# Stacks of five chunks made by PE and ACT, and one chunk's look-up moved to the seam of two tiles

## The chip, the core and the metric

The kernel runs on one core of one Trainium2 chip. Its engines are PE (TensorE, matrix products), DVE (VectorE), ACT (ScalarE), POOL (GpSimd) and SP (SyncE, which here only issues DMAs). The metric is the device time of one execution in microseconds (us), lower is better.

## What is computed

A recommendation tower for 2048 rows: 39 table look-ups of 32 numbers, a bilinear form for each of the 741 pairs of fields, and a three-layer perceptron.

```python
e = jnp.stack([tbl_0[ids[:, 0]], ..., tbl_38[ids[:, 38]]], axis=1)   # 2048 x 39 x 32
p = inputs[:, ROW, :]                                                # inputs is e; ROW < COL, all pairs
q = inputs[:, COL, :]
z = jnp.einsum('bpc,apc,bpa->bp', p, w, q)                           # w: 32 x 741 x 32
h = jnp.concatenate([z, dense_ctx], axis=1)                          # 741 + 16 columns
h = jnp.maximum(h @ W_top1 + b_top1, 0.0)
h = jnp.maximum(h @ W_top2 + b_top2, 0.0)
y = h @ W_top3
```

## The kernel before

The 2048 rows are four tiles of 512 (tile 0 to 3). The 39 fields are ten chunks of four (chunk 9 has three). A chunk of a tile is written (tile, chunk), as (1, 8).

**Units and batches.** The pairs are 200 units per tile. A unit is one PE product of a weight block with the stack of one field j (`interact`, L593), multiplied by DVE with the plain form of a chunk (`multiply`, L914, two units at a time: one product, 100 per tile), and summed into z by PE (`reduce`, L617). Two products make a batch; there are 50 batches per tile, and this document numbers them through, so that batch 69 is batch 19 of tile 1. PE's order in a batch is: the four matmuls of `interact`, pieces of the perceptron of the tile before (L630, L632), `reduce` of the batch before, then a turn or look-ups for chunks to come.

**How a chunk is brought.** Either its rows are gathered by POOL, one DMA for each field and 128 rows (L422), and turned by PE (`turn`, L537); or it is looked up: DVE makes one-hot rows of the indices (L902), one slice at a time, and PE multiplies them with the table (`look_up`, L556; 12 matmuls for a full slice of four fields, ten slices for chunks 1, 7 and 8). Both end in the PSUM buffer `t_ps`, which has one place. ACT then copies it twice (`take_chunk`, L720 and L725): a rounded high part `parts`, and the plain form `eT`. DVE subtracts for the low part (`split_chunk`, L868).

**How a stack is made.** `interact` needs for each field both parts repeated over all 128 partitions, in `e4`. SP does it through DRAM: `store_parts` writes the high part (L467) and the low part (L469) to `scratch`, and `stack_chunk` reads them back, repeated (L480, two DMAs of 512 KB), after it has waited for both stores. All of it stands in SP's one queue, with the pieces of the weights (L439) and the indices (L459). For the first chunks of tile 0 (`MADE`: chunks 1, 0, 2, 3, 7) it is done without DRAM: `make_half` (L574) multiplies the parts with a repeating matrix into PSUM, two fields at once, and ACT copies the result into `e4` (L735 to L738).

**What sets the order.** Tables written by hand: `FIRST_TILE` and `OTHER_TILES` give for each chunk the batch of its turn, or one batch for each slice of its look-up (batches of 50 and more are those of the next tile). The stores and stacks follow from the batch in which the chunk is complete: the store one batch later, the stack two batches later (three or four in tile 0), but not before the stack that has the place in `e4` is used up. `UNITS` sets when a stack is first needed: chunk 1 and 0 in batch 0 of a tile, 2 in batch 2, 3 in batch 5, 7 in batch 9, 4 in batch 14, 8 in the second product of batch 19, 5 in 28, 6 in 36, 9 in 42. POOL's gathers each wait, up to number 96, for the landing of the third gather before; after that they are paced by the products done.

**Places in `eT`.** Chunks 0, 1, 2, 3 and 7 have two, so the next tile's can be written while this tile's is still in use; the others have one, and wait for the last product of the tile before.

Of the kernel before, what the change touches and what calls it, by code (L numbers as in the profile page):

```python
# [5 lines left out]
P = 128  # L6
F = 39
D = 32
# [13 lines left out]
def fields_in(g):  # L22
    return min(C, F - C * g)
# [72 lines left out]
def place_sums():  # L96
# [3 lines left out]
    for (g, gi, j), quad in zip(UNITS, map(int, QUADS)):  # L100
# [4 lines left out]
        if quad == 0 and D * (NZ - 1) <= row < D * (NZ - 1) + DENSE:  # L105
# [20 lines left out]
OS = 3  # L126
PR = 4

TWO_PLACES = (0, 1, 2, 3, 7)

# [11 lines left out]
FIRST_TILE = ((2, 0, 0, (0, 0, 0, 1, 1, 1, 1, 1)), (7, 0, None, (1, 1, 1, 2, 2, 2, 2, 2, 2, 2)), (3, 0, 3, ()), (4, 0, 7, ()),  # L142
# [3 lines left out]
OTHER_TILES = ((8, 0, None, (0, 1, 1, 2, 3, 4, 4, 5, 6, 6)), (4, 0, 7, ()),  # L146
# [3 lines left out]
LAST_TABLE_BATCH = 2  # L150

MADE = ((0, 1), (0, 0), (0, 2), (0, 3), (0, 7))
MADE_FIRST = 2
MADE_IN = {1: (((0, 2), 0), ((0, 2), 1)), 4: (((0, 3), 0), ((0, 3), 1)), 5: (((0, 7), 0),), 6: (((0, 7), 1),)}
MLP_WEIGHTS_BATCH = 7
LATE = (17, 39)
# [32 lines left out]

def stores_to(n):  # L190

    return len([m for m in range(n + 1) if (m - n) % 2 == 0 and ORDER[m] not in MADE])


def halves_before(c, half):
# [34 lines left out]
    INDICES.setdefault(LAST_SLICE.get(LOOKED[LPOS[c] - 2], -1) + 1, []).append(c)  # L230
for b, cs in COMPLETE.items():
    for c in cs:
        if c in MADE:
            continue
        x = e4_before(c)
        free = NBAT * x[0] + J_LAST[x[1]] // UPB + 1 if x else 0

        late = LATE[0] <= b < LATE[1]
        STORES.setdefault(b + 1 + late, []).append(c)
        STACKS.setdefault(max(b + (4 if late else 3 if b < LATE[0] else 2), free), []).append(c)  # L240
# [43 lines left out]
def tower(nc, tables, ids, hot_ids, hot_rows, dense, w, w1, b1, w2, b2, w3, sel_in, ident_in, y):  # L284
# [4 lines left out]
    with ExitStack() as ctx:  # L289
# [229 lines left out]
        def _(pe):  # L519
# [42 lines left out]
            def make_half(c, half):  # L562
# [12 lines left out]
                                                start=h == 0, stop=h == 1)  # L575
                last.then_inc(s_stk, 1)

            def interact(t, n):
                s = NS * t + n
                if s >= 2:  # L580
                    pe.wait_ge(s_mul, s - 1)
                slots = [e_slot(t, UNITS[UPS * n + i][1]) for i in range(UPS)]
                for i in range(UPS):
                    u = UPS * n + i
                    g, gi, j = UNITS[u]
                    if u == J_FIRST[g]:
                        pe.wait_ge(s_e4[E4_SLOT[g]], 32 * e4_loads((t, g)))
                    if u % PW == 0:
                        p = NPW * t + u // PW
                        pe.wait_ge(s_w4[p % WR], 16 * (p // WR + 1))  # L590
                    place = i if slots[0] <= slots[1] else 1 - i
                    p = NPW * t + u // PW
                    last = nc.tensor.matmul(u_ps[:, s % 2, place, :], w4[:, p % WR, (u % PW) * P:(u % PW + 1) * P],  # L593
                                            e4[:, E4_SLOT[g], j - C * g, :], start=True, stop=True)
                last.then_inc(s_u, 1)
# [86 lines left out]
            for t in range(NT):  # L682
                for b in range(NBAT):
                    for x in range(SPB):
                        interact(t, SPB * b + x)
                    if t:
                        for piece in mlp_pieces(b, t == NT - 1):
                            mlp_piece(t - 1, *piece)
                    if b:
                        reduce(t, b - 1)  # L690
                    elif t:
                        reduce(t - 1, NBAT - 1)
                    for c in TURNS.get(NBAT * t + b, ()):
                        turn(c)
                    for c, k in TAKES.get(NBAT * t + b, ()):
                        look_up(c, k)
                    if t == 0:
                        for c, half in MADE_IN.get(b, ()):
                            make_half(c, half)
                    if t == NT - 1:  # L700
                        for m, k in EARLY.get(b, ()):
                            early_piece(t, m, k)
# [3 lines left out]
        def _(act):  # L706
            def take_chunk(c):
# [1 line left out]
                n = POS[c]  # L709
                rows = D * fields_in(g)  # L710
                if n >= 2:
                    if ORDER[n - 2] in MADE:
                        act.wait_ge(s_stk, 2 * MADE.index(ORDER[n - 2]) + 2)
                    else:
                        act.wait_ge(s_scr[n % 2], 32 * stores_to(n - 2))
                if hot(c):
# [9 lines left out]

            def take_half(c, half):
                made = MADE.index(c)
                act.wait_ge(s_stk, 2 * made + half + 1)
                x = e4_before(c)  # L730
                if x:
                    act.wait_ge(s_u, step_after(*x))
# [3 lines left out]
                else:  # L736
                    nc.scalar.copy(e4[:, slot, q, :], m_ps[:, :]).then_inc(s_e4[slot], 8)
                    nc.scalar.copy(e4[:, slot, q + 1, :], z_ps[:, 1, :]).then_inc(s_e4[slot], 8)  # L738

            def load_weights(k):  # L740
                a, b = PREP_UNITS[k]
# [86 lines left out]
            for t in range(NT):  # L828
                for b in range(NBAT):
                    if t:  # L830
                        for layer, m, k in mlp_pieces(b, t == NT - 1):
                            if k == LAYER_INPUTS[layer] - 1:
                                take_mlp(t - 1, layer, m, m_ps[:, :])
                    for tile in range(NZ):
                        done = ends_tile(tile) // UPB + 1
                        if done == b:
# [189 lines left out]
```

## Time and profile before

| | |
|---|---|
| median of 3 runs | 739.4 us (738.17 to 740.45) |
| the profiled execution: its own time | 739.08 us |
| its span, first to last instruction | 737.2 us |
| PE busy | 678.2 us, 92% |
| DVE busy | 608.3 us, 83% |
| ACT busy | 104.3 us, 14% |
| POOL busy | 415.6 us, 56% |

The two busiest engines are PE and DVE, and they hand work to each other in every batch. A mean share hides the stages: the profile's 40 slices show PE at 6 to 9 tenths in the first twelve or so, and at 9 in nearly all that follow, while the share of the DMA engines is highest in the slices from 74 to 203 us. The span is 1.9 us shorter than the execution's own time.

### The profile page before, as it was taken

The page shows a single profiled execution, that of the slowest core. Times are in us where ns is not written, and L with a number is a line of the kernel's source. Part 1 is how long each engine was busy: PE and PEld are TensorE (multiplying, and loading weights), DVE is VectorE, ACT ScalarE, POOL GpSimd, SP SyncE. Part 2 cuts the span into 40 slices and gives each one's busy share as a digit, 9 for nine tenths or more (in the row PEclk, how much of TensorE's full clock was granted, in tenths as well). Part 3 has the DMA queues.
Part 4 walks back from the last instruction along what each step waited for, and adds up shares of the span by engine and source line. Part 5 has one row for each costly group of instructions (what it writes and reads, how often), then busy time and mean ns, then how long its engine had stood idle before and what let it go on. Part 6 is the DMA issues. An engine that isn't in the chain of part 4 may idle for free.

```text
span 737.2 us, 10924 instructions
## 1 busy us (share of the span) xinstructions
PE 678.2 (92%) x4202; PEld 274.6 (37%) x4202; DVE 608.3 (83%) x773; ACT 104.3 (14%) x186; POOL 415.6 (56%) x424
## 2 busy tenths in 40 slices
PE   0678886898997999999999999999999999999998
PEld 0233332333333444434344444433434444343443
DVE  3776797799996998898889997998889978788740
ACT  3423301111110010101211010110110101011002
POOL 5777465567777766567766665567766666000000
PEclk9888999899998999999999999999999999999999
DMA  7644979779876573547675582728686373553200
GB/s 200 209 119 138 334 272 301 252 231 314 284 227 202 195 257 108 166 140 236 224 225 192 202 281 68 240 85 259 194 270 214 125 254 98 179 174 104 97 0 0
DMA packets 72271, 141.40 MB, mean 192 GB/s; under 512 B 13829, under 2 KB 23704, under 8 KB 72092
## 3 DMA queue, kind: packets, MB, share of 16 engines
q1 hardware_dynamic: 48796, 116.86, 46.2%
q10 hardware_dynamic: 9984, 16.94, 6.4%
q0 software_dynamic: 13440, 6.91, 6.4%
q8 instruction: 33, 0.54, 0.3%
q14 instruction: 18, 0.15, 0.1%
HBM read 109.66 MB, written 31.00 MB: 191 GB/s over the span
## 4 chain that ended last, share of the span: by engine, by line
PE 70%; DVE 14%; issue 7%; DMA 4%; POOL 3%; ACT 1%; SPq 0%; DVEq 0%; ACTq 0%
PE u_ps L593 23%; PE z_ps L617 21%; DVE prod L914 9%; PE m_ps L630 8%; PE t_ps L556 7%; DVE one_hot L902 4%; POOL e_rows L422 3%; PE m_ps L632 3%; PE t_ps L537 2%; DMA e<-scratch 1%; DMA e_rows<-in_tbl_dram,idx 1%; PE u_ps L652 1%; PE u_ps L661 1%; PE m_ps L634 1%; PE t_ps L644 1%
## 5 line engine op out<-in xcount | busy, mean ns | idle before, releaser
L422 POOL DMA_INDIRECT e_rows<-in_tbl_dram,idx x420 | 415.4, 989 | 212.9 <-issue 89.9
L914 DVE TENSOR_TENSOR prod<-u_ps,eT 128x1024 f32<-128x1024 f32 x400 | 469.5, 1216 | 77.6 <-PE u_ps L593 77.1
L593 PE MATMUL u_ps<-e,w 128*128 128x512 f32 x800 | 260.9, 437 | 24.6 <-DVE prod L914 14.6
L617 PE MATMUL z_ps<-prod,sel 128*32 128x512 f32 x1600 | 222.9, 614 | 0.0
L593 PEld LDWEIGHTS u_ps<-e,w 128*128 128x128 f32 x800 | 132.2, 190 | 173.4 <-DVE prod L914 85.9
L902 DVE TENSOR_SCALAR one_hot<-hot_idx,row 125x512 bf16<-125x512 f16 (+2 forms) x296 | 107.6, 420 | 9.6 <-PE t_ps L556 5.8
L556 PE MATMUL t_ps<-one_hot,tb 125*32 125x512 bf16 x1344 | 104.2, 392 | 10.5 <-DVE one_hot L902 9.1
L556 PEld LDWEIGHTS t_ps<-one_hot,tb 125*32 125x32 bf16 x1344 | 43.7, 99 | 89.3 <-issue 57.6
L617 PEld LDWEIGHTS z_ps<-prod,sel 128*32 128x32 f32 x1600 | 33.8, 108 | 111.7 <-issue 87.4
L630 PE MATMUL m_ps<-zT,w1s 128*128 128x512 f32 x144 | 73.5, 592 | 0.0
L720 ACT CAST parts<-t_ps 128x512 fp32r<-128x512 f32 (+1 forms) x40 | 23.4, 586 | 295.4 <-PE t_ps L556 162.4
L868 DVE TENSOR_TENSOR parts<-eT,parts 128x512 fp32r<-128x512 f32 (+1 forms) x40 | 27.3, 683 | 3.2 <-ACT eT L725 3.2
L630 PEld LDWEIGHTS m_ps<-zT,w1s 128*128 128x128 f32 x144 | 27.2, 189 | 6.4
L791 ACT ACTIVATE h<-m_ps,b1s 128x512 f32<-128x512 f32 x13 | 9.0, 689 | 145.1 <-PE m_ps L630 143.9
L784 ACT COPY zT<-z_ps 128x512 f32<-128x512 f32 x24 | 14.1, 586 | 102.9 <-PE z_ps L617 102.9
L537 PE MATMUL t_ps<-ident,e_rows 128*128 128x128 f32 (+2 forms) x112 | 19.2, 296 | 6.6 <-DMA e_rows<-in_tbl_dram,idx 6.6
L632 PE MATMUL m_ps<-h,w2s 128*128 128x512 f32 x48 | 24.5, 592 | 0.0
L725 ACT COPY eT<-t_ps 128x512 f32<-128x512 f32 (+1 forms) x40 | 23.7, 591 | 0.0
L537 PEld LDWEIGHTS t_ps<-ident,e_rows 128*128 128x128 f32 (+2 forms) x112 | 12.2, 142 | 30.3 <-issue 27.1
L875 DVE TENSOR_TENSOR h<-h 128x512 fp32r<-128x512 f32 (+1 forms) x13 | 8.7, 668 | 2.7 <-ACT h L751 2.7
L751 ACT CAST h<-h 128x512 fp32r<-128x512 f32 (+1 forms) x13 | 7.9, 609 | 17.2 <-DMA h<-in_w_dram 17.2
L632 PEld LDWEIGHTS m_ps<-h,w2s 128*128 128x128 f32 x48 | 9.0, 188 | 2.1
(52 smaller groups left out, 122.2 us busy)
## 6 DMA issues: line engine op xcount, KB each, us to landing
w<-w_rows SPq DMA_DIRECT2D x100, 512.0 KB
e<-scratch SPq DMA_DIRECT2D x62, 512.0 KB, 5.7
scratch<-parts SPq DMA_DIRECT2D x62, 256.0 KB
w_rows<-h ACTq DMA_DIRECT2D x48, 256.0 KB
e_rows<-in_tbl_dram,idx POOLq DMA_INDIRECT x420
hot_idx<-hot SPq DMA_DIRECT2D x12, 512.0 KB
h<-in_w_dram ACTq DMA_DIRECT2D x12, 256.0 KB, 4.3
e<-scratch SPq DMA_DIRECT2D x8, 384.0 KB
```

The lines of the kernel that those rows point to most:

```text
L422: pool.indirect_dma_start(e_rows[:, r, n, D * q:D * q + D], None, tables[f], bass.IndirectOffsetOnAxis(ap=idx[:, t, f * TPG + n:f * TPG + ...
L537: last = nc.tensor.transpose(t_ps[0:hi, b * P:b * P + P], rows, ident[:, :])
L556: last = nc.tensor.matmul(t_ps[D * q:D * q + D, :], tb[0:HP, part, col:col + D], one_hot[0:HP, n % OS, here * NB:(here + 1) * NB], start=k ...
L593: last = nc.tensor.matmul(u_ps[:, s % 2, place, :], w4[:, p % WR, (u % PW) * P:(u % PW + 1) * P], e4[:, E4_SLOT[g], j - C * g, :], start=T ...
L617: last = nc.tensor.matmul(z_ps[D * quad:D * quad + D, z % 2, :], sel[:, D - 1 - row:2 * D - 1 - row], prod[:, (NS * t + n) % PR, place, :] ...
L630: last = nc.tensor.matmul(m_ps[:, :], w1s[:, k, m * P:m * P + P], zT[:, t % 2, k, :], start=k == 0, stop=stop)
L632: last = nc.tensor.matmul(m_ps[:, :], w2s[:, k, m * P:m * P + P], h1[:, k, :], start=k == 0, stop=stop)
L720: nc.scalar.copy(parts[0:rows, n % 2, 0, :], t_ps[0:rows, :]).then_inc(s_eh, 1)
L725: nc.scalar.copy(eT[0:rows, e_slot(t, g), :], t_ps[0:rows, :]).then_inc(s_et, 1)
L868: nc.vector.tensor_tensor(parts[0:rows, n % 2, 1, :], eT[0:rows, e_slot(t, g), :], parts[0:rows, n % 2, 0, :].bitcast(F32), ALU.subtract). ...
L902: last = nc.vector.tensor_scalar(one_hot[0:HP, n % OS, i * NB:(i + run) * NB], hot_idx[0:HP, LPOS[c] % 2, x * NB:(x + run) * NB], (row10 i ...
L914: nc.vector.tensor_tensor(prod[:, s % PR, :, :], u_ps[:, s % 2, :, :], e, ALU.mult).then_inc(s_mul, 1)
```

## The change

Three things are changed.

1. The stacks of (0, 4), (0, 8), (0, 5), (0, 6) and (0, 9) no longer pass through DRAM. `FIELD_WISE` gives the first batch of each; in that batch and the following ones `make_field` has PE repeat one field by two matmuls into `m_ps`, between `interact` and `reduce`, and `take_field` has ACT copy it into `e4`. That is 19 fields in batches 9 to 12, 15 to 18, 21 to 24, 30 to 33 and 35 to 37.
2. The look-up of the next tile's chunk 7 moves to batches 46 to 52 (48 to 52 in tile 0), where it was in 20 to 27 (32 to 38). In the other tiles chunk 8 moves behind chunk 4, from batches 0 to 6 to batches 8 to 15, and the others by some batches: the turn of chunk 5 from 19 to 16, chunk 9 from 36 to 34, the next tile's chunk 2 from 39 to 37, 0 from 43 to 41, 3 from 49 to 45; the look-up of the next tile's chunk 1 from 8 to 17 to 17 to 26.
3. Chunk 7 has one place in `eT`.

```diff
-TWO_PLACES = (0, 1, 2, 3, 7)
+TWO_PLACES = (0, 1, 2, 3)
...
-              (7, 1, None, (32, 32, 33, 33, 34, 35, 35, 36, 37, 38)), (2, 1, 40, ()), (0, 1, 43, ()), (3, 1, 48, ()))
-OTHER_TILES = ((8, 0, None, (0, 1, 1, 2, 3, 4, 4, 5, 6, 6)), (4, 0, 7, ()),
...
+              (2, 1, 40, ()), (0, 1, 43, ()), (3, 1, 48, ()), (7, 1, None, (48, 49, 49, 49, 50, 50, 51, 51, 52, 52)))
+OTHER_TILES = ((4, 0, 7, ()), (8, 0, None, (8, 9, 10, 10, 11, 12, 13, 13, 14, 15)), (5, 0, 16, ()),
...
+FIELD_WISE = {(0, 4): 9, (0, 8): 15, (0, 5): 21, (0, 6): 30, (0, 9): 35}
+STACKED = MADE + tuple(FIELD_WISE)
...
 for b, cs in COMPLETE.items():
     for c in cs:
-        if c in MADE:
+        if c in STACKED:
             continue
...
+            def make_field(c, q):
+
+                n = POS[c]
+                pe.wait_ge(s_el, n + 1)
+                d = c if q else STACKED[STACKED.index(c) - 1]
+                pe.wait_ge(s_e4[E4_SLOT[d[1]]], 32 * e4_loads(d) - (32 - 8 * q if q else 0))
+                own = slice(D * q, D * q + D)
+                for h in range(2):
+                    last = nc.tensor.matmul(m_ps[:, :], rep[own, 2 - 2 * h:2 - 2 * h + P], parts[own, n % 2, h, :],
+                                            start=h == 0, stop=h == 1)
+                last.then_inc(s_stk, 1)
...
                     for x in range(SPB):
                         interact(t, SPB * b + x)
+                    if t == 0:
+                        for c, q in field_in(b):
+                            make_field(c, q)
...
+            def take_field(c, q):
+                act.wait_ge(s_stk, stk_at(c, q))
+                act.wait_ge(s_u, step_after(*e4_before(c)))
+                slot = E4_SLOT[c[1]]
+                rest = 8 if q < fields_in(c[1]) - 1 else 32 - 8 * q
+                nc.scalar.copy(e4[:, slot, q, :], m_ps[:, :]).then_inc(s_e4[slot], rest)
```

**Place 1: PE in tile 0, the batches from 15.** `u_ps` is the result of `interact`, `z_ps` that of `reduce`, `m_ps<-parts,rep` a repeated field. Before:

```order
L593 MATMUL u_ps<-e,w 128x512 x4
L617 MATMUL z_ps<-prod,sel 32x512 x4
L593 MATMUL u_ps<-e,w 128x512 x4
L617 MATMUL z_ps<-prod,sel 32x512 x4
L593 MATMUL u_ps<-e,w 128x512 x4
```

In the changed kernel:

```order
L622 MATMUL u_ps<-e,w 128x512 x4
L603 MATMUL m_ps<-parts,rep 128x512 x2
L646 MATMUL z_ps<-prod,sel 32x512 x4
L622 MATMUL u_ps<-e,w 128x512 x4
L603 MATMUL m_ps<-parts,rep 128x512 x2
L646 MATMUL z_ps<-prod,sel 32x512 x4
L622 MATMUL u_ps<-e,w 128x512 x4
L603 MATMUL m_ps<-parts,rep 128x512 x2
```

Batch 15 and batch 16 have each got the two matmuls of one field of chunk 8 between `interact` and `reduce`, and so have 17 and 18.

**Place 2: SP in tile 1, from the first store of (1, 8).** `scratch<-parts` is a store, `e<-scratch` a stack's read, `hot_idx<-hot` the indices of a look-up, `w<-w_rows` a piece of the weights. Before, the second pair of stores is that of (1, 4):

```order
L467 DMA scratch<-parts 128x512 [waits s_eh]
L469 DMA scratch<-parts 128x512 [waits s_el]
L459 DMA hot_idx<-hot 128x2048 [waits s_hot]
L467 DMA scratch<-parts 128x512 [waits s_eh]
L469 DMA scratch<-parts 128x512 [waits s_el]
L480 DMA e<-scratch 64x4x512 [waits s_scr1,s_u]
L480 DMA e<-scratch 64x4x512
```

In the changed kernel, the second pair is that of (1, 5):

```order
L484 DMA scratch<-parts 128x512 [waits s_eh]
L486 DMA scratch<-parts 128x512 [waits s_el]
L456 DMA w<-w_rows 128x1024 [waits s_u]
L476 DMA hot_idx<-hot 128x2048 [waits s_hot]
L484 DMA scratch<-parts 128x512 [waits s_eh]
L486 DMA scratch<-parts 128x512 [waits s_el]
L497 DMA e<-scratch 64x4x512 [waits s_scr0,s_u]
L497 DMA e<-scratch 64x4x512
L497 DMA e<-scratch 64x4x512 [waits s_scr1,s_u]
L497 DMA e<-scratch 64x4x512
```

The order is the same but for one piece of the weights: the stack of (1, 8) stands behind both stores of the next chunk, and the next chunk's stack follows at once.

**Place 3: PE, from the last slice of chunk 8's look-up.** `t_ps<-one_hot,tb` is a look-up, `t_ps<-ident,e_rows` a turn, `m_ps<-zT,w1s` a piece of the perceptron. Before, in tile 2, where the row of 18 is the end of the look-up of (2, 8), in batch 106:

```order
L556 MATMUL t_ps<-one_hot,tb 32x512 x18
L593 MATMUL u_ps<-e,w 128x512 x4
L630 MATMUL m_ps<-zT,w1s 128x512
L617 MATMUL z_ps<-prod,sel 32x512 x4
L537 MATMUL t_ps<-ident,e_rows 128x128 x4
L593 MATMUL u_ps<-e,w 128x512 x4
L630 MATMUL m_ps<-zT,w1s 128x512
L617 MATMUL z_ps<-prod,sel 32x512 x4
L556 MATMUL t_ps<-one_hot,tb 32x512 x12
L593 MATMUL u_ps<-e,w 128x512 x4
L630 MATMUL m_ps<-zT,w1s 128x512
```

In the changed kernel, in tile 1, where the two rows of 9 are its end, in batches 64 and 65:

```order
L573 MATMUL t_ps<-one_hot,tb 32x512 x9
L622 MATMUL u_ps<-e,w 128x512 x4
L659 MATMUL m_ps<-zT,w1s 128x512
L646 MATMUL z_ps<-prod,sel 32x512 x4
L554 MATMUL t_ps<-ident,e_rows 128x128 x4
L622 MATMUL u_ps<-e,w 128x512 x4
L659 MATMUL m_ps<-zT,w1s 128x512
L646 MATMUL z_ps<-prod,sel 32x512 x4
L573 MATMUL t_ps<-one_hot,tb 32x512 x12
L622 MATMUL u_ps<-e,w 128x512 x4
L659 MATMUL m_ps<-zT,w1s 128x512
L646 MATMUL z_ps<-prod,sel 32x512 x4
L573 MATMUL t_ps<-one_hot,tb 32x512 x12
L622 MATMUL u_ps<-e,w 128x512 x4
```

The batches behind the look-up hold the same work. What moved is the first use of the stack: before it is in batch 119, thirteen batches behind the row of 18; now it is in the last row shown, four batches behind the second row of 9 (the third and fourth matmul of that `interact`).

## Rows read from the trace of the kernel before

**Rows 1.** Windows: stretch, length, busy (count) of PE, PEld, DVE, ACT, POOL; PEclk, DMA.
```profile
39.40:234.00 194.60, 165.31 (x1146) 62.01 (x1145) 167.79 (x226) 31.32 (x56) 130.27 (x128) 0.93 0.74 246
234.00:395.50 161.50, 160.85 (x1023) 67.12 (x1022) 145.58 (x182) 18.49 (x33) 107.09 (x112) 1.00 0.62 197
...
127.40:134.20 6.80, 3.17 (x11) 0.89 (x12) 1.94 (x4) 0.00 (x0) 3.53 (x4) 0.50 0.74 262
...
226.40:233.20 6.80, 4.98 (x17) 2.50 (x18) 3.00 (x4) 1.07 (x2) 4.97 (x7) 0.50 0.40 135
```

**Rows 2.** Waits, whole run: engine, line, cause, total us, times, longest.
```profile
PE u_ps L593 <- DMA e<-scratch: 5.8, 1, 5.8
```

**Rows 3.** Windows of product L914: stretch, length, busy (count), clock, DMA.
```profile
125.40:135.10 9.70, 2.56 (x3) 0.65 0.82 302
175.50:198.80 23.30, 16.39 (x14) 1.00 0.92 317
201.70:212.20 10.50, 9.32 (x8) 1.00 0.59 184
```

**Rows 4.** Timeline at 119 to 132 us: start, length, engine, line, operation.
```profile
119.64 1.35 SPq L480 DMA_DIRECT2D e<-scratch  x2
...
131.03 1.19 PE L593 MATMUL u_ps<-e,w 128*128 128x512 f32 x2 [5.76 <-DMA e<-scratch]
```

**Rows 5.** Timeline at 221 to 229 us.
```profile
221.96 0.94 POOL L422 DMA_INDIRECT e_rows<-in_tbl_dram,idx  x1 [0.30 <-issue]
...
228.22 1.09 PE L537 MATMUL t_ps<-ident,e_rows 128*128 128x128 f32 x4 [4.13 <-DMA e_rows<-in_tbl_dram,idx]
```

**Rows 6.** Gathers L422, 4 to 159 us: wait, total us, times.
```profile
  DMA e_rows<-in_tbl_dram,idx: 33.0, 25
```

**Rows 7.** Timeline at 81 to 83 us: stacks made by PE.
```profile
81.98 0.50 PE L574 MATMUL m_ps<-parts,rep 32*128 32x512 f32 x1
...
82.65 0.73 PE L593 MATMUL u_ps<-e,w 128*128 128x512 f32 x2
```

**Rows 8.** Chain of waits at 266 us: start, length, work.
```profile
266.77 0.99 PE z_ps L617 x8
267.77 0.65 PE t_ps L556 x12
```

**Rows 9.** Timeline at 256 to 269 us: chunk 8 of tile 1.
```profile
256.29 1.48 PE L556 MATMUL t_ps<-one_hot,tb 125*32 125x512 bf16 x18
...
261.45 0.32 SPq L469 DMA_DIRECT2D scratch<-parts  x1
...
264.54 0.68 DVE L868 TENSOR_TENSOR parts<-eT,parts 128x512 fp32r<-128x512 f32 x1
...
265.13 1.01 DVE L902 TENSOR_SCALAR one_hot<-hot_idx,row 125x512 bf16<-125x512 f16 x3
...
268.35 1.21 PE L593 MATMUL u_ps<-e,w 128*128 128x512 f32 x4
```

**Rows 10.** Stack line L480 at 265 us: issues, issue to landing.
```profile
L480 SPq DMA_DIRECT2D e<-scratch x2: 592/615/638, 265.7 to 266.3; - x2
...
DMA to landing us min/median/max: 5.5/6.1/6.7
```

**Rows 11.** L480 at 427 us, and PE's timeline at 430 us.
```profile
L480 SPq DMA_DIRECT2D e<-scratch x2: 592/614/637, 427.7 to 428.3; - x2
...
DMA to landing us min/median/max: 5.0/5.4/5.9
...
430.34 1.21 PE L593 MATMUL u_ps<-e,w 128*128 128x512 f32 x4
```

**Rows 12.** L480 at 589 us, and PE's timeline at 591 us.
```profile
L480 SPq DMA_DIRECT2D e<-scratch x2: 592/608/625, 589.3 to 590.0; - x2
...
DMA to landing us min/median/max: 5.2/5.6/5.9
...
591.12 1.20 PE L593 MATMUL u_ps<-e,w 128*128 128x512 f32 x4
```

More of the change, by code:

```diff
@@ L144 @@
               (1, 1, None, (20, 21, 22, 22, 23, 24, 25, 25, 26, 27)), (6, 0, 28, ()), (9, 0, 31, ()),
[1 row of a table removed]
-OTHER_TILES = ((8, 0, None, (0, 1, 1, 2, 3, 4, 4, 5, 6, 6)), (4, 0, 7, ()),
[3 rows of a table removed]
[1 row of a table added]
+OTHER_TILES = ((4, 0, 7, ()), (8, 0, None, (8, 9, 10, 10, 11, 12, 13, 13, 14, 15)), (5, 0, 16, ()),
+               (1, 1, None, (17, 18, 19, 20, 21, 22, 23, 24, 25, 26)), (6, 0, 28, ()), (9, 0, 34, ()),
+               (2, 1, 37, ()), (0, 1, 41, ()), (3, 1, 45, ()), (7, 1, None, (46, 47, 47, 48, 49, 49, 50, 51, 51, 52)))
 LAST_TABLE_BATCH = 2
@@ L190, in stores_to, with stk_at, stk_after, field_in @@
 def stores_to(n):
-    return len([m for m in range(n + 1) if (m - n) % 2 == 0 and ORDER[m] not in MADE])
+    return len([m for m in range(n + 1) if (m - n) % 2 == 0 and ORDER[m] not in STACKED])
+def stk_at(c, part):
+    earlier = STACKED[:STACKED.index(c)]
+    return sum(2 if x in MADE else fields_in(x[1]) for x in earlier) + part + 1
+def stk_after(c):
+    return stk_at(c, (2 if c in MADE else fields_in(c[1])) - 1)
+def field_in(b):
+    return [(c, b - first) for c, first in FIELD_WISE.items() if first <= b < first + fields_in(c[1])]
 def halves_before(c, half):
@@ L711, in take_chunk @@
                 if n >= 2:
-                    if ORDER[n - 2] in MADE:
-                        act.wait_ge(s_stk, 2 * MADE.index(ORDER[n - 2]) + 2)
+                    if ORDER[n - 2] in STACKED:
+                        act.wait_ge(s_stk, stk_after(ORDER[n - 2]))
                     else:
@@ L728, in take_half @@
                 made = MADE.index(c)
-                act.wait_ge(s_stk, 2 * made + half + 1)
+                act.wait_ge(s_stk, stk_at(c, half))
                 x = e4_before(c)
@@ L833, in _ @@
                                 take_mlp(t - 1, layer, m, m_ps[:, :])
+                    if t == 0:
+                        for c, q in field_in(b):
+                            take_field(c, q)
                     for tile in range(NZ):
```

3 rows, old and new, of the table OTHER_TILES are left out of this document.

## The prediction

> **What bounds the kernel now.** I read first the windows by tile, then the list of waits, then the timeline at each long wait, and last the timeline where the work stands that the change moves.
>
> The windows show two regimes [rows 1]. In tile 1 (tiles 2 and 3 are alike) PE is busy for all but 0.7 us, at a granted clock of 1.00, which is 2.4 GHz: PE bounds, and a wait of PE there is added to the time in full. Tile 0 takes 194.6 us against 161.5 for tile 1, though no perceptron runs beside it. So tile 0 has something to give back.
>
> The waits say that PE waits for a stack's DMA once in the whole run [rows 2]. The timeline shows where: at the second product of batch 19, the first use of chunk 8, PE stands idle 5.76 us until 131.03; its stack was issued at 119.64 [rows 4]. A second idle of 4.13 us ends at 228.22: the turn of (1, 3) in batch 48 waits for its last gather, issued at 221.96, with POOL issuing back to back at 0.30 us gaps [rows 5]. After each of the two the clock is at 0.50, 1.2 GHz, for 6.8 us [rows 1]: it fell 2.1 us after the first idle began (125.3) and 2.3 us after the second (224.1).
>
> **The change, part by part.** The sum is made against the profiled execution's own time, 739.1 us (span 737.2), which is 0.3 under the median of the runs.
>
> *Chunk 8's stack in tile 0.* The stretch from the first product of batch 19 to that of batch 20 is 9.7 us [rows 3]. A batch with little beside it takes 10.5 / 4 = 2.6 (the stretch 201.7 to 212.2, eight products). The fourth field is made in batch 18, with a `reduce` and two matmuls between it and its use, so nothing is late: 7.1 us go, the half clock among them.
>
> *Nineteen fields on PE.* A `make_half` puts four matmuls on PE in 82.65 - 81.98 = 0.67 us; `m_ps` and `z_ps` run side by side there [rows 7]. A single field is two matmuls behind one another in the same row group, so 0.67 as well: 12.7 us if all of it shows. But in tile 0 DVE is the busier engine (167.8 against 165.3 us), and in 2.6 us of a light batch PE has some 2.1 of work: `reduce` is 0.99 [rows 8], and the four matmuls of `interact` 1.1 to 1.2 [rows 9]. With a field it needs 2.8. So some 0.2 to 0.4 us shows for each, and next to nothing where slices of a look-up keep DVE busy at 1.01 each [rows 9]. I take 0.3: +5.7 us, between 0 and 12.7. The 19 copies cost nothing: ACT is busy 31.3 of 194.6 us.
>
> At this place the Trainium skill speaks against the change. "TensorEngine Tiling", Key Properties, says that changing the tiling mode, not merely the tile, drains TensorE; each field has 32 rows between work of another shape, so two such changes each. By the rule 38 drains would be added; as one matmul is reported at 0.50 us and its half of the 0.67 is 0.34, that is 0.16 each, 6.1 us, and the sum below would be 757. The trace does not show it: the row at 82.65 begins with no gap behind the fields [rows 7].
>
> *The look-up of (1, 7) leaves batches 32 to 38.* They take 23.3 us for seven; at 2.6 they would be 18.2: -5.1.
>
> *The turn of (1, 3).* It would be wanted at 224.1 - 7.1 - 5.1 + 5.7 = 217.6. For that its gathers must come 10 us sooner. Of the first 96 gathers 25 waited for landings, 33.0 us in all [rows 6], beside the stores and stacks that go (5 x 1.5 MB) and the weights that stay. Bounds are 0 and 33; I take 10, a third of it, since only part of the waits stand beside those stacks. The turn is then at 218.
>
> *The end of tile 0.* From that turn to tile 1's first product (234.0) it is now 5.8 us, 5.0 of them at half clock, of which 2.5 are lost. Added are four slices of (1, 7), at 1.01 us on DVE: 5.8 - 2.5 + 4.0 = 7.3. Tile 1 starts at 225.3: tile 0 gives -8.7 us.
>
> *Looks moved to later tiles.* A full slice of twelve matmuls is 0.65 us of PE [rows 8]. 24 matmuls more fall to tile 1 and 30 to tile 3: 54 x 0.054 = 2.9. At the seams two slices in a batch cost DVE 2.0 beside two products, more than PE's share; but batches 0 to 6 are so filled today. I take +3.0 for all of this, between 0 and 6.
>
> *Chunk 8 in tiles 1 to 3: what is late next.* Now the look-up ends in batch 15 of the tile and the stack is needed in batch 19. Today's trace holds this very sequence, nine batches earlier, with the same work on PE and SP behind it, so the lateness can be read. In tile 1 the look-up ends at 256.29 + 1.48 = 257.8; DVE's split comes behind the next batch's products, and the low part's store is issued at 261.45. The stack stands in SP's queue behind the low store of the next chunk, whose split starts at 264.54 [rows 9]. It is issued at 265.7 and 266.3 and the later one lands 6.7 us after: at 273.0 [rows 10]. The chain takes 15.2 us. PE is at the second product of the fourth batch behind the look-up half way through the row of four at 268.35, at 269.0. Lateness: 4.0 us. In the same way tile 2: 428.3 + 5.9 = 434.2 against 430.9, 3.3 [rows 11]; tile 3: 590.0 + 5.9 = 595.9 against 591.7, 4.2 [rows 12]. Today nobody sees it, since chunk 8 is needed nine batches later. Behind the waiting matmul stand the perceptron's pieces, `reduce`, every look and turn, and DVE waits for u: nothing is caught up in a tile that PE bounds. +11.5 us, between 8 (each later read landing in 5.0 us, the least in these rows) and 16 (the piece of weights that now stands ahead of the stack, up to 1.5 each).
>
> The Trainium skill's "DMA: Bandwidth & Descriptors", Bandwidth, gives 6.15 us for a transfer of 1 MB. The stack is two reads of 512 KB; by that figure it would land at 265.7 + 6.15 = 271.8 in tile 1, 2.9 us late, not 4.0, and the sum would be some 3 us lower. The rows have 7.3 us from the first issue, and they decide.
>
> *The clock behind those stalls.* The two long idles of today were followed by 6.8 us at half, beginning 2.1 to 2.3 us into the idle. A stall of 4.0 would leave 5.0 us of work at half, 2.5 lost; three make 7.5, or 0 if the clock stays. The new stalls are a little shorter than the two in the rows, except by 0.1 in one: I take 2.0 each, +6.0.
>
> **Sum.** 739.1 - 8.7 + 3.0 + 11.5 + 6.0 = 750.9, so 751 us.
>
> **Rivals.** *The stacks are there in time* (faster). If SP reaches them sooner or the tile runs slower up to batch 19, no stall appears and the time is 739.1 - 8.7 + 3.0 = 733. It decides where the chain from the end of the look-up to the landing is under 11 us. For it: in tile 2 the pair landed 6.5 us after the first issue, in tile 1 7.3, so it varies. Against: the two stores and the split alone took 8 us before the first issue, and three rows out of three are late.
>
> *The stalls come, the clock stays*: 739.1 - 8.7 + 3.0 + 11.5 = 745. For: they are short. Against: the clock fell at 2.1 and 2.3 us of idle.
>
> *POOL holds tile 0.* If the gathers get nothing back, the turn of (1, 3) stays at 228, and tile 0 ends at 228 + 7.3 + 2.5 = 238, so 12.5 us more than in my sum: 763; with half of it 757. For: POOL issues there at 0.94 + 0.30 = 1.24 us each [rows 5], which no freed DMA shortens. Against: the 33.0 us of waits.
>
> *The drains*, 757, see above.
>
> *The change does not take the stall of batch 19 away*, since ACT's copies are late. ACT is idle most of the tile, and the last copy has a `reduce` to itself. Then 758.
>
> **Chances.** Forecast (stalls with a falling clock) 0.60, with a range of its own of 746 to 757; stalls with the clock kept 0.15; in time 0.12; POOL 0.08; drains 0.03; the last 0.02. The range of 8 in 10 is 738 to 760: it leaves out most of the rival in time, and the worst of POOL's. A measurement tells 0.3%, 2.2 us, from no change. Faster by over that: 0.13, the rival in time and a little of the kept clock with shorter stalls; within it 0.04; slower 0.83.
>
> **What would show it.** Right: among the waits, PE at `interact` for the stack's DMA three times, 3 to 5 us each, in tiles 1, 2 and 3, at the second product of batches 69, 119 and 169, each with a stretch at clock 0.50; tile 0 at about 186 us, with no stall at batch 19; DVE still the busier one there. Wrong: tiles 1 to 3 without such waits; the turn in batch 48 idle for over 3 us; tile 0 over 192 us, which would say that the fields cost more than 0.3 each.

## The result, and the profile after

The changed kernel takes 756.1 us (median of 4 runs, 753.9 to 759.7). The kernel before, on the same chip, takes 738.8 us (4 runs, 736.8 to 740.5). The ratio is 1.025, with a 95% interval of 1.021 to 1.028. The forecast was 751 us, slower, with a range of 738 to 760. It was 5 us low, which the point-by-point section takes apart.

The profiled execution took 757.1 us, 18.0 more than the one before. The page of the changed kernel, the lines that answer to the numbers shown of before:

```profile
span 755.3 us, 11032 instructions
...
PE 694.4 (92%) x4240; PEld 282.8 (37%) x4240; DVE 610.0 (81%) x773; ACT 115.2 (15%) x205; POOL 412.4 (55%) x424
...
DMA packets 68304, 133.94 MB, mean 177 GB/s; under 512 B 13509, under 2 KB 23384, under 8 KB 68124
...
L622 PE MATMUL u_ps<-e,w 128*128 128x512 f32 x800 | 259.8, 439 | 26.9 <-DMA e<-scratch 13.9
...
L777 ACT CAST e<-m_ps 128x512 fp32r<-128x512 f32 x19 | 11.2, 587 | 60.1 <-PE m_ps L603 59.3
...
L603 PE MATMUL m_ps<-parts,rep 32*128 32x512 f32 x38 | 14.8, 471 | 0.0
```

The engines' shares have hardly moved, and 7.5 MB fewer pass through the DMA engines. Neither tells of a slower kernel. One number in the fifth part does: 13.9 us in which PE waited for stacks. The 19 fields are there as well (L603, L777).

The windows of the changed kernel by tile, then four stretches at half clock (columns as in [rows 1]):

```profile
39.90:228.00 188.10, 172.82 (x1133) 67.22 (x1133) 163.96 (x216) 41.12 (x73) 130.79 (x132) 0.93 0.66 210
228.00:399.40 171.40, 164.34 (x1045) 68.25 (x1043) 147.60 (x185) 18.96 (x33) 104.19 (x108) 0.98 0.60 191
399.40:567.90 168.50, 162.19 (x1023) 67.30 (x1022) 146.87 (x183) 18.97 (x33) 104.23 (x109) 0.99 0.59 190
...
116.80:127.00 10.20, 10.20 (x30) 3.84 (x29) 5.41 (x5) 1.17 (x2) 6.40 (x7) 0.50 0.41 128
297.70:304.50 6.80, 5.82 (x24) 1.87 (x24) 2.14 (x4) 0.00 (x0) 1.20 (x1) 0.50 0.85 308
468.30:471.70 3.40, 3.40 (x12) 1.00 (x14) 2.14 (x4) 0.00 (x0) 1.20 (x1) 0.51 1.05 388
635.60:639.00 3.40, 3.40 (x12) 0.85 (x10) 1.23 (x1) 0.00 (x0) 0.94 (x1) 0.50 0.93 343
```

Tile 0 gave back 6.5 us (194.6 before [rows 1], 188.1 now). Each later tile is longer: tile 1 by 9.9 (161.5 before [rows 1]), tile 2 by 6.5, tile 3, counted to the end of the span, by 7.7 (the table below has all of them). Taken between the first products of the tiles, with 0.5 us before tile 0, that is 0.5 - 6.5 + 24.1 = 18.1.

The stretch of one batch in which the stack of chunk 8 is first needed, from the windows of the product's line: tiles 1, 2 and 3, then tile 0, then the last five batches of tile 1 (stretch, length, busy, clock, DMA share, GB/s):

```profile
293.40:305.30 11.90, 2.43 (x2) 0.71 0.72 259
463.80:473.40 9.60, 2.43 (x2) 0.82 0.90 321
630.90:640.10 9.20, 2.45 (x2) 0.81 0.95 336
132.00:135.20 3.20, 2.36 (x2) 1.00 0.96 277
381.50:399.30 17.80, 11.75 (x10) 1.00 0.62 206
```

In tile 0 that batch took 9.7 us [rows 3] and now takes 3.2: the stall is gone. In the later tiles it took 3.3, 3.3 and 3.4 us in the kernel before and now takes 11.9, 9.6 and 9.2, 20.7 us more in all. The rest of the three tiles is 3.4 us longer. The seam shows on its own: 17.8 us for five batches, where the kernel before has

```profile
381.10:395.40 14.30, 11.69 (x10) 1.00 0.68 215
```

That is 3.5 us more, with two slices of a look-up and two products on DVE in a batch. The first eight batches of tile 1, now free of chunk 8's slices, give 2.6 of it back (28.3 us before, 25.7 after).

The waits of the changed kernel, whole run, which answer to [rows 2]:

```profile
PE u_ps L622 <- DMA e<-scratch: 13.9, 3, 5.4
```

Three waits now stand where there was one of 5.8. The timeline of PE and SP in tile 1, from the end of the look-up of (1, 8) on (start, length, engine, line, operation, idle before it and what ended it). It is the sequence that [rows 9] had nine batches earlier:

```profile
281.17 0.83 PE L573 MATMUL t_ps<-one_hot,tb 125*32 125x512 bf16 x9
...
285.68 0.32 SPq L486 DMA_DIRECT2D scratch<-parts  x1
...
286.04 0.43 SPq L456 DMA_DIRECT2D w<-w_rows  x1
...
286.52 0.46 SPq L476 DMA_DIRECT2D hot_idx<-hot  x1
...
289.47 0.32 SPq L486 DMA_DIRECT2D scratch<-parts  x1
289.88 7.53 SPq L497 DMA_DIRECT2D e<-scratch  x4
...
298.68 1.19 PE L622 MATMUL u_ps<-e,w 128*128 128x512 f32 x2 [5.37 <-DMA e<-scratch]
299.67 1.91 PE L659 MATMUL m_ps<-zT,w1s 128*128 128x512 f32 x2
```

The look-up ends at 282.0, and the low part's store is issued at 285.68. The stack may go only at 289.88, behind the next chunk's low store at 289.47 (of the four reads in that row the first two are this stack, the others the next chunk's). PE stands idle for 5.37 us, and the matmuls that follow take 1.91 us for two where 1.02 is usual. In tiles 2 and 3 the same matmul ends idles of 4.26 and 4.30:

```profile
468.02 0.90 PE L622 MATMUL u_ps<-e,w 128*128 128x512 f32 x2 [4.26 <-DMA e<-scratch]
```
```profile
635.30 0.92 PE L622 MATMUL u_ps<-e,w 128*128 128x512 f32 x2 [4.30 <-DMA e<-scratch]
```

The stack's line in tile 1, which answers to [rows 10]:

```profile
L497 SPq DMA_DIRECT2D e<-scratch x2: 592/712/832, 289.9 to 290.5; - x2
...
DMA to landing us min/median/max: 5.7/6.9/8.0
```

The later of the two reads landed 8.0 us after its issue, at 298.5; it was 6.7 in [rows 10]. The whole chain, end of look-up to landing, is 298.5 - 282.0 = 16.5 us. I had read 15.2 for it.

### The profile page after: what moved, and what is told of

It is laid out like the page before. It is cut to its first block, busy times and chain, and to the rows that moved or that the text cites. A ratio compares the mean times of both kernels' runs of the same rounds, so it can differ in the third digit from the quotient of the medians.

```text
span 755.3 us, 11032 instructions
## 1 busy us (share of the span) xinstructions
PE 694.4 (92%) x4240; PEld 282.8 (37%) x4240; DVE 610.0 (81%) x773; ACT 115.2 (15%) x205; POOL 412.4 (55%) x424
## 4 chain that ended last, share of the span: by engine, by line
PE 67%; DVE 14%; issue 7%; DMA 5%; POOL 4%; ACT 1%; SPq 0%; DVEq 0%; ACTq 0%
PE u_ps L622 22%; PE z_ps L646 20%; DVE prod L956 10%; PE m_ps L659 8%; PE t_ps L573 6%; POOL e_rows L439 4%; DVE one_hot L944 4%; DMA e<-scratch 3%; PE m_ps L661 2%; DMA e_rows<-in_tbl_dram,idx 2%; PE t_ps L554 2%; PE u_ps L681 1%; PE m_ps L603 1%; PE u_ps L690 1%; PE t_ps L673 1%
## 5 line engine op out<-in xcount | busy, mean ns | idle before, releaser
L622 PE MATMUL u_ps<-e,w 128*128 128x512 f32 x800 | 259.8, 439 | 26.9 <-DMA e<-scratch 13.9
L646 PE MATMUL z_ps<-prod,sel 128*32 128x512 f32 x1600 | 225.5, 620 | 0.0
L622 PEld LDWEIGHTS u_ps<-e,w 128*128 128x128 f32 x800 | 134.0, 192 | 174.7 <-issue 89.4
L573 PE MATMUL t_ps<-one_hot,tb 125*32 125x512 bf16 x1344 | 102.1, 387 | 12.0 <-DVE one_hot L944 9.3
L659 PE MATMUL m_ps<-zT,w1s 128*128 128x512 f32 x144 | 76.2, 611 | 0.0
L554 PEld LDWEIGHTS t_ps<-ident,e_rows 128*128 128x128 f32 (+2 forms) x112 | 11.8, 139 | 28.0 <-issue 23.0
L777 ACT CAST e<-m_ps 128x512 fp32r<-128x512 f32 x19 | 11.2, 587 | 60.1 <-PE m_ps L603 59.3
L603 PE MATMUL m_ps<-parts,rep 32*128 32x512 f32 x38 | 14.8, 471 | 0.0
```

Of the source, the lines that this page charges most:

```text
L554: last = nc.tensor.transpose(t_ps[0:hi, b * P:b * P + P], rows, ident[:, :])
L573: last = nc.tensor.matmul(t_ps[D * q:D * q + D, :], tb[0:HP, part, col:col + D], one_hot[0:HP, n % OS, here * NB:(here + 1) * NB], start=k ...
L646: last = nc.tensor.matmul(z_ps[D * quad:D * quad + D, z % 2, :], sel[:, D - 1 - row:2 * D - 1 - row], prod[:, (NS * t + n) % PR, place, :] ...
L659: last = nc.tensor.matmul(m_ps[:, :], w1s[:, k, m * P:m * P + P], zT[:, t % 2, k, :], start=k == 0, stop=stop)
```

## The experiments

Six kernels were run. Two theories were on the table. A: the stack of chunk 8 comes too late in tiles 1 to 3, because its chain has a length of its own and too few batches to fit in, and the clock falls in the wait. B, in several forms: the rest of the change, the moved look-ups, the fields or the traffic, has a good part in it. The table gives all results; "stretch" is the batch in which chunk 8 is first needed. The lengths in it are of the one profiled execution of each kernel. The runs of the kernel before beside the six had medians of 737.9 us (19 runs) and, for the one batch sooner and the filled wait, 738.3 (13). The changed kernel's four runs stand beside the 738.8, so a difference to its median carries up to 0.9 us by which these three differ, and its own spread of 6.

| kernel | median us (runs) | ratio to before, 95% | tiles 0 to 3, us | stretch in tiles 1, 2, 3 |
|---|---|---|---|---|
| before | 738.8 (4) | | 194.6, 161.5, 162.0, 179.6 | 3.3, 3.3, 3.4 |
| changed | 756.1 (4) | 1.021 to 1.028 | 188.1, 171.4, 168.5, 187.3 | 11.9, 9.6, 9.2 |
| chunk 8 three batches sooner | 736.3 (10) | 0.997 to 1.002 | 185.1, 163.2, 161.8, 181.0 | 3.7, 3.7, 3.0 |
| chunk 8 one batch sooner | 739.8 (10) | 0.999 to 1.005 | 190.0, 164.8, 163.6, 182.5 | 4.8, 5.1, 4.5 |
| stack first in SP's queue | 753.0 (4) | 1.017 to 1.027 | 185.2, 166.3, 169.2, 188.3 | 7.0, 8.7, 10.1 |
| wait filled with matmuls | 750.4 (4) | 1.011 to 1.026 | 188.4, 167.7, 166.2, 185.6 | 8.3, 7.7, 7.4 |
| tables alone, no fields | 762.3 (4) | 1.027 to 1.041 | 193.6, 171.6, 167.6, 187.0 | 11.1, 9.2, 8.9 |
| fields alone, old tables | 734.9 (10) | 0.993 to 0.999 | 187.2, 161.4, 162.0, 179.6 | 3.4, 3.4, 3.4 |

**Chunk 8 three batches sooner.** The whole change stays, but in the later tiles chunk 8 is looked up three batches earlier, and the turn of chunk 4 makes room.

```diff
-OTHER_TILES = ((4, 0, 7, ()), (8, 0, None, (8, 9, 10, 10, 11, 12, 13, 13, 14, 15)), (5, 0, 16, ()),
+OTHER_TILES = ((4, 0, 4, ()), (8, 0, None, (5, 6, 7, 7, 8, 9, 10, 10, 11, 12)), (5, 0, 16, ()),
```

> The changed kernel with one table line altered: in tiles 1 to 3 chunk 4 is turned in batch 4 (not 7) and chunk 8 is looked up in batches 5 to 12 (not 8 to 15), so its stack has seven batches, not four, before its first use. Theory A (the loss of the changed kernel is the three waits of PE for chunk 8's stack, 5.4 + 4.3 + 4.3 us, with the half clock behind them): no such wait is left, the stretches from the first product of batches 69, 119 and 169 to the next fall from 11.9, 9.6 and 9.2 us to about 3.4 each, 20 us in all, and the time is 736 (734 to 739). Rival B (the loss is the two slices in a batch at the seams and the dense look-ups, which keep DVE busy): the waits may go but the time stays over 748.

Measured: 736.3 us, and no wait of PE for a stack in the list of waits. The three stretches, windows of the product's line:

```profile
290.00:293.70 3.70, 2.37 (x3) 1.00 0.93 313
452.20:455.90 3.70, 2.39 (x3) 1.00 0.94 325
612.70:615.70 3.00, 2.35 (x2) 1.00 0.67 220
```

This is theory A with its number. One row of a table carries the whole loss: 19.8 us between the medians. The first two of these stretches have a DMA share as high as or higher than in the changed kernel (0.93 against 0.72 in tile 1, 0.94 against 0.90 in tile 2), so a high share in that batch makes no stall by itself.

The row does more than give room. In the changed kernel the stack is issued 4.2, 4.2 and 3.8 us behind its low store, after both stores of the next chunk; here no other chunk's store stands between, and it goes 2.1 us behind. From the low store to the landing of the later read it takes 9.6, 9.6 and 7.3 us in the three tiles, against 12.9, 11.8 and 10.5. So the chain itself is shorter here, and this experiment does not separate the three batches of room from that. The last experiment, a single batch with the next chunk's stores still ahead of the stack, comes nearer to it.

**The stack first in SP's queue.** Within a batch SP now issues the stack before the next chunk's stores.

```diff
-                    for c in STORES.get(NBAT * t + b, ()):
-                        store_parts(c)
                     for c in STACKS.get(NBAT * t + b, ()):
                         stack_chunk(c)
+                    for c in STORES.get(NBAT * t + b, ()):
+                        store_parts(c)
```

> The changed kernel with SP's two loops of a batch swapped: stacks due in a batch are issued ahead of the stores due in it. Theory A (part of the lateness is the place in SP's queue, behind both stores of the next chunk): the stack of chunk 8 is issued as soon as its own low store has landed, about 2.2 us sooner, each of the three waits gets 2.2 us shorter, and the time falls by 6 to 10, to 746 to 750. Rival B (the DMA engines' traffic sets the landing, not the place in the queue): the stack lands when it did, the waits stay at 13.9 us in sum, and the time stays at 756 within 1.5.

Measured: 753.0 us, 3 less than the changed kernel, where 6 to 10 were expected; the medians alone can't tell 3 us here, the traces can. The timeline in tile 1:

```profile
282.38 0.32 SPq L486 DMA_DIRECT2D scratch<-parts  x1
...
284.86 1.25 SPq L497 DMA_DIRECT2D e<-scratch  x2
...
293.25 0.70 PE L622 MATMUL u_ps<-e,w 128*128 128x512 f32 x2 [3.23 <-DMA e<-scratch]
```

The first read goes out 2.5 us behind the low store, not 4.2. It helps only in part: from the low store to the matmul that waits it now takes 10.9, 10.9 and 10.8 us in the three tiles, against 13.0, 11.9 and 10.6 in the changed kernel. In tile 3 nothing was gained. Its place in the queue is worth about 2 us in tile 1 and 1 in tile 2. What remains is two passes through DRAM behind each other; how the 10.8 us divide into the store, the reads and the traffic beside them was not tried. The expectation was half right: the issue came sooner in all three tiles, as theory A had it, and the landing followed in two.

Part of the gain is hidden. In tile 2 of this trace the turn of (3, 3) waited for its gather, and 3.4 us at half clock began there, at 544.0, which the changed kernel does not have:

```profile
543.74 0.85 PE L554 MATMUL t_ps<-ident,e_rows 128*128 128x128 f32 x4 [2.00 <-DMA e_rows<-in_tbl_dram,idx]
```

That is why tile 2 is no shorter here than in the changed kernel, though its stretch is.

**Fields alone.** `FIRST_TILE`, `OTHER_TILES` and the two places of chunk 7 are those of before; the five chunks' stacks are still made by PE and ACT.

```diff
-TWO_PLACES = (0, 1, 2, 3)
+TWO_PLACES = (0, 1, 2, 3, 7)
...
-OTHER_TILES = ((4, 0, 7, ()), (8, 0, None, (8, 9, 10, 10, 11, 12, 13, 13, 14, 15)), (5, 0, 16, ()),
...
+OTHER_TILES = ((8, 0, None, (0, 1, 1, 2, 3, 4, 4, 5, 6, 6)), (4, 0, 7, ()),
```

> The kernel before with the field-wise stacks alone: old tables, two places for chunk 7. Theory A (fields cost 0.3 us each, the wait at batch 19 goes, and POOL's gathers come sooner so that the turn of batch 48 waits no more): 739 - 7.1 + 5.7 - 6.6 = 731 (728 to 734). Rival B (what the changed kernel's trace shows in batches 16 to 19, a stretch of 10.2 us at half clock with no long idle, belongs to the fields and comes back here): tile 0 gains only 1 to 4 us, 735 to 738.

Measured: 734.9 us. Tile 0 and tile 1, and the batch of chunk 8 in tiles 0 and 1, windows of the product's line:

```profile
39.50:226.70 187.20, 117.03 (x101) 0.96 0.66 216
226.70:388.10 161.40, 117.41 (x101) 1.00 0.60 196
128.60:131.80 3.20, 2.35 (x2) 1.00 0.97 277
293.70:297.00 3.30, 2.34 (x2) 1.00 0.68 200
```

Tiles 1 to 3 are those of before to 0.1 us, and tile 0 is 7.4 shorter. Between the medians the gain is 3.0. Neither expectation was met: theory A had 728 to 734, rival B 735 to 738, and 734.9 lies between them. The 7.4 is that of the fastest of the ten executions, the one that was profiled (731.5 us). Three of the ten had a mean granted clock of 0.984 and took 731.5 to 731.9 us; the seven at 0.974 to 0.979 took 734.0 to 737.9. So the trace shows an execution with little half clock, and the gain of the kernel is nearer to 3.0. This version is faster than both kernels, than the one before by 0.4%, which the interval just keeps apart from nothing.

**Tables alone.** The fields go back to DRAM; the tables stay changed.

```diff
-FIELD_WISE = {(0, 4): 9, (0, 8): 15, (0, 5): 21, (0, 6): 30, (0, 9): 35}
+FIELD_WISE = {}
```

> The changed kernel without field-wise stacks: new tables and one place for chunk 7, the five stacks of tile 0 again through DRAM. Theory A (the tables bring the whole loss in tiles 1 to 3, 24 us; tile 0 is as before, with its waits in batches 19 and 48, and four slices more at its end): 762 to 766. Rival B (the fields carry part of the loss, by way of ACT or PE): 756 or less.

Measured: 762.3 us. The two waits of tile 0 are back, at the first use of chunk 8 and at the turn of (1, 3):

```profile
PE u_ps L622 <- DMA e<-scratch: 15.7, 4, 5.0
```
```profile
223.58 1.09 PE L554 MATMUL t_ps<-ident,e_rows 128*128 128x128 f32 x4 [5.01 <-DMA e_rows<-in_tbl_dram,idx]
```

The first of these lines holds the one in tile 0, 2.8 us, beside those of tiles 1 to 3. So the tables cost 762.3 - 737.9 = 24.4 us by themselves, as theory A had it, and the fields give 3.0 alone and 762.3 - 756.1 = 6.2 beside the tables; these two are differences of medians that spread by as much. It also shows that the stall of (1, 3)'s turn goes with the fields and not with the moved look-up: without the fields it is 5.0 us long, with them the turn does not wait.

**The wait filled.** In front of the wait in tiles 1 to 3 PE does 16 matmuls on data that is there, into the place that the waiting product then overwrites. The result is unchanged and no wait is taken away.

```diff
+FILL = 16
...
+                    if u == J_FIRST[8] and t > 0:
+                        p = NPW * t + (u - 1) // PW
+                        for k in range(FILL):
+                            nc.tensor.matmul(u_ps[:, s % 2, i, :], w4[:, p % WR, ((u - 1) % PW) * P:((u - 1) % PW + 1) * P],
+                                             e4[:, E4_SLOT[7], 0, :], start=True, stop=True)
```

> The changed kernel with 16 more matmuls on PE in front of each of the three waits for chunk 8's stack: their results are overwritten, and they end before the stack lands, so the stack's wait costs what it did (5.4, 4.3 and 4.3 us in sum of fill and idle), but PE is busy in it. Theory A (of the 20 us that the three places cost, 14 are the idle itself and some 6 the half clock behind it): the clock stays at 1.00 there, and the time falls by 4 to 7, to 749 to 752. Rival B (the 6 us beyond the idle are PE and DVE getting back into step, not the clock): no change, or slower by up to 2 us.

Measured: 750.4 us, 5.7 less than the changed kernel, with 48 matmuls more. The timeline in tile 1, and the stretches of the three tiles:

```profile
293.57 3.83 PE L619 MATMUL u_ps<-e,w 128*128 128x512 f32 x16
...
298.26 0.73 PE L628 MATMUL u_ps<-e,w 128*128 128x512 f32 x2 [0.85 <-DMA e<-scratch]
298.83 1.02 PE L665 MATMUL m_ps<-zT,w1s 128*128 128x512 f32 x2
```
```profile
293.90:302.20 8.30, 2.41 (x2) 1.00 0.97 333
460.50:468.20 7.70, 2.43 (x2) 1.00 0.96 335
625.20:632.60 7.40, 2.45 (x2) 1.00 0.99 344
```

The stack lands nearly as late as in the changed kernel (12.1, 11.5 and 10.4 us behind its low store, against 12.9, 11.8 and 10.5), but the granted clock stays at 1.00, and the two matmuls behind the wait take 1.02 us and not 1.91. The stretches lose 3.6, 1.9 and 1.8 us: 7.3 in the profiled executions, of which 1.0 is the sooner landing and 6.3 the clock. Between the medians of four runs it is 5.7. This separates the two parts of the stall: the wait itself, and the half clock behind it, about 6 us of the 17.

**Chunk 8 one batch sooner.** Between the changed kernel and the first experiment.

```diff
-OTHER_TILES = ((4, 0, 7, ()), (8, 0, None, (8, 9, 10, 10, 11, 12, 13, 13, 14, 15)), (5, 0, 16, ()),
+OTHER_TILES = ((4, 0, 6, ()), (8, 0, None, (7, 8, 9, 9, 10, 11, 12, 12, 13, 14)), (5, 0, 15, ()),
```

> The changed kernel with the turns of chunks 4 and 5 and the look-up of chunk 8 one batch sooner in tiles 1 to 3 (6, 7 to 14, 15): the same order, also in SP's queue, with five batches in place of four between the look-up and the use. Theory A (a chain of fixed length against batches of 3.65 us in tiles 1 and 2 and 3.0 in tile 3): the waits fall to 1.7, 0.6 and 1.3 us, the half clock goes with them, and the time is 738 to 742. Rival B (the chain is not of fixed length but goes with the traffic and POOL's pacing around batch 19): the waits shrink by less than 2 us each and the time stays over 746.

Measured: 739.8 us. The list of waits, the waiting matmul in tile 3, and the stretches:

```profile
PE u_ps L622 <- DMA e<-scratch: 2.1, 2, 1.2
```
```profile
622.58 0.70 PE L622 MATMUL u_ps<-e,w 128*128 128x512 f32 x2 [1.34 <-DVE prod L956]
```
```profile
295.00:299.80 4.80, 2.48 (x3) 1.00 1.04 395
459.00:464.10 5.10, 2.45 (x3) 1.00 1.05 396
621.30:625.80 4.50, 2.42 (x2) 1.00 1.05 396
```

The list has two of the three waits. The third, 1.34 us in tile 3, it puts down to DVE; but the stack landed there at 622.44, 0.14 us before the matmul, as in the other tiles, so it is the stack's too. The waits are 0.9, 1.2 and 1.3 us, where theory A had 1.7, 0.6 and 1.3. A batch there is about 3.5 us (281.94 to 285.33 to 288.94 in the changed kernel), and the waits shrink from 13.9 in sum to 3.5, by 3.5 each: a chain of nearly the same length, whose start was moved. From the low store to the landing it is 11.4, 11.7 and 10.5 us, against 12.9, 11.8 and 10.5. One thing in SP's queue is not as in the changed kernel, against what was expected: the piece of the weights goes behind the stack (289.47 in tile 1, after the reads at 288.14 and 288.78), as in the kernel before. The clock does not fall at these waits, so one batch of room is worth 756.1 - 739.8 = 16.3 us.

## Why the prediction was right, and where it was off

**The sign and the mechanism** were right: PE waits for the stack of chunk 8 at batches 69, 119 and 169, each time with a stretch at half clock. Moving that look-up and the turns beside it by one batch brings the kernel back to 739.8, by three to 736.3. Two of the signs named did not come: tile 0 took 188.1 us, not about 186, and PE and not DVE is the busier engine in it, 172.8 us against 164.0; the matmuls of the fields and the half clock are both in that number.

**Lateness of the stack.** The forecast had 4.0, 3.3 and 4.2 us, 11.5 in sum. The trace has 5.4, 4.3 and 4.3, 13.9 in sum. The mis-sized step is the landing, not the queue. From the end of the look-up to the first issue it took 289.9 - 282.0 = 7.9 us, as in [rows 9, 10]. But the later read took 8.0 us to land where [rows 10] had 6.7, 6.9 in tile 2 where [rows 11] had 5.9, and 6.1 in tile 3 where [rows 12] had 5.9. A piece of the weights is now issued ahead of the stack in all three tiles, as the upper bound of this term had foreseen with up to 1.5 us each; the landings went up by 1.3, 1.0 and 0.2. With chunk 8 one batch sooner that piece stands behind the stack, and the later read takes 6.9, 7.3 and 6.1 us: less than in the changed kernel in tile 1 alone. So the piece is not the whole cause, and what is stays open.

**The clock behind it.** The forecast had 2.0 each, 6.0. The trace has stretches of 6.8, 3.4 and 3.4 us. All of the last two and 5.8 of the first are work, so half of them is lost: 2.9 + 1.7 + 1.7 = 6.3, and the filled wait, worth 5.7 us between the medians, agrees. But that the 6.0 came out right is partly luck: the working was wrong in two places that cancelled. The clock fell 4.4 us after the idle of tile 1 began (293.3 to 297.7), and 4.5 and 4.6 in the others. I had 2.1 to 2.3 from [rows 1, 4, 5]. And it stayed low for 3.4 us twice, not for 6.8.

**Chunk 8's stack in tile 0.** The forecast was that 7.1 us go. The batch takes 3.2 instead of 9.7: 6.5. The mechanism is right and the size is 0.6 off: there is no field in batch 19, but a turn, and it is not the light batch of 2.6 us that the sum took.

**Nineteen fields on PE.** I took 0.3 us each, 5.7 in sum. The kernel with the fields alone takes 60.4 us for batches 28 to 47 of tile 0, with seven fields, where the kernel before takes 59.1: 0.2 each. The other twelve are cheaper. Batches 9 to 12 take 15.7 us for 15.6, batches 15 to 18 12.6 for 10.0, of which 1.7 is half clock, and batches 20 to 24 19.0 for 19.3. In sum the 19 cost about 2 us, a third of what I took. A field in the changed kernel, timeline of PE:

```profile
129.71 0.73 PE L603 MATMUL m_ps<-parts,rep 32*128 32x512 f32 x2
130.37 1.07 PE L646 MATMUL z_ps<-prod,sel 128*32 128x512 f32 x8
```

It holds PE for 0.66 us (129.71 to 130.37), and most of that lies beside DVE.

**Batches 32 to 38 and the turn of (1, 3).** With the tables alone the seven batches take 18.3 us, where I had 18.2; with five fields in them they take 19.7. The gathers' waits in the same stretch as [rows 6]:

```profile
  DMA e_rows<-in_tbl_dram,idx: 24.9, 25
```

That is 8.1 us less than 33.0; I had taken 10. The turn comes at 219.85, where I had 218, and does not wait. Before, it stood idle for 4.13 us until 228.22 [rows 5].

**Tile 0 as a whole** gave 6.5 us, where the sum said 8.7. What the sum lacked is one stretch, batches 15 to 18, at the clock of 0.50 from 116.8 to 127.0. PE was busy in all of the 10.2 us, so up to half of it is lost, 5.1. That is more than the 2.2 that are missing; the fields, 3.7 us cheaper than I took them, make up for it, with small differences elsewhere. The kernel with the fields alone has 3.4 us there, the kernel before none. This term was not in the sum at all. The four batches take 10.0 us in the kernel before; among the six kernels with the fields, 12.5, 12.5 and 12.6 us where the stretch is 3.4 us long, and 15.5 each where it is 10.2. But each of these is one execution, and executions of one kernel differ in their granted clock as much as these kernels do (last section). So how much of the 6.5 us belongs to the kernel and how much to the execution is not shown.

**Looks moved to later tiles.** Forecast +3.0, measured +3.4 outside the three stretches. Right, and in tile 1 the seam alone is 3.5, the first batches -2.6.

**The sum** was 751 for 756. The profiled execution says where the 6.2 us between its 757.1 and my 750.9 are: 2.2 in tile 0, 2.4 in the waits, 0.3 in the clock, 0.4 in the other looks and 0.5 ahead of tile 0, which is 5.8; the 0.4 left lies in the three stretches, beside the waits.

**The rivals.** *In time* fell: no tile of the three was in time. The first experiment shows that its number, 733, was a fair one (736.3). *The clock kept* fell by the traces; the filled wait, at 750.4, is what it would have looked like. *POOL holds tile 0* fell: the turn does not wait. It is not far off, though. With the tables alone the wait is 5.0 us and the gathers wait 31.5 us in all, so the relief came with the fields; that it is because they take stores and stacks off the DMA engines is likely and was not tried by itself. *The drains* fell. By "TensorEngine Tiling", Key Properties, of the Trainium skill they would have added, by the prediction's estimate, 6.1 us to the fields' 5.7. The measured fields cost less than the 5.7 without them, and the row at 130.37 follows the field with no idle. So this case's trace gives no sign of that rule, though a small cost could hide in it: a field's two matmuls take 0.66 us, and the four of `interact` before them 1.14 (128.57 to 129.71), so two of those take 0.57. *The stall of batch 19 stays* fell, by the 3.2 us of that batch.

The Trainium skill's 6.15 us for 1 MB ("DMA: Bandwidth & Descriptors", Bandwidth) would have made the stack less late. The trace has 298.5 - 289.9 = 8.6 us in tile 1, from the first issue to the landing. The rows of before, with 7.3, were nearer and still too low.

## What to carry to other kernels

Measure a chain through DRAM (split, store, queue, read) from the end of its source to its landing, and count the batches to its first use: here it took 16.5 us in tile 1, and one batch more of room was worth 16 us. The chain can be read from the trace of before, in any place where nobody waits for it. But it is not of one length: with nothing of the next chunk ahead of it in the queue, its part behind the low store was 2 to 3 us shorter. Where two edits come together, run each alone: here one was a gain and the other cost 24 us.

## What was not expected of the hardware

- How soon the clock falls in an idle and how long it stays low is not fixed. Before, it fell 2.1 and 2.3 us into two idles and stayed low for 6.8. Here it fell 4.4 to 4.6 us after idles of 5.4, 4.3 and 4.3 began, and was low for 6.8, 3.4 and 3.4. Idles of 1.2 and 1.3 us (one batch sooner) left it at 1.00. With the stack first in the queue an idle of 3.2 us left it there too, and one of 3.3 was followed by 3.4 us at half, as was one of only 2.0 before a turn. A rule for the moment it falls is not shown by these runs.
- The clock also fell where PE had no idle of more than 1.5 us, at about 117 us in tile 0. In the profiled executions it was 3.4 us long in four of the kernels, 10.2 in three and absent in the kernel before. The kernel without the fields has it as well (3.4 us), so they are not its cause by themselves. It moves tile 0 by some 3 us between its two lengths, and why it comes at one or the other stays open. The length may well change from one execution of a kernel to the next: only one of each was traced.
- Executions of the same kernel on one core spread by more than the forecast's 0.3%: the kernel before from 733.1 to 742.0 us in 13. In the changed kernel's runs the time goes with the mean granted clock (755.2 us at 0.971, 757.1 at 0.968, 759.7 at 0.966), and so it does with the fields alone (731.5 to 731.9 at 0.984, 734.0 to 737.9 at 0.974 to 0.979). In the kernel before it does so only loosely (734.2 at 0.977, 738.4 at 0.981). Only with 10 runs of one and 19 of the other could 734.9 be told from 737.9. A single traced execution can be 3 us off its kernel's median: that of the fields alone is.
